# Source one-hots of the edge count split by columns between VectorE and ScalarE, beside a GpSimd scatter

## The reference

```
deg = segment_sum(ones, dst)                    # edges that end in each node
for k in 1, 2, 3:
    agg = segment_sum((feat * d_invsqrt)[src], dst)
    feat = feat - agg * d_invsqrt
    h = h + THETA[k] * feat
```

## Time and profile before

| | |
|---|---|
| median of 3 runs | 6393.17 us (6391.6 to 6401.1) |
| the profiled execution: its time, its span | 6387.14 us, 6385.3 us |
| TensorE matmul, weight load | busy 65% and 43% of the span |
| VectorE, ScalarE, GpSimd | busy 50%, 12% and 52% |
| scatter L440 | 784 instructions, 379.7 to 1493 us |
| counting | 419.5 to 931 us |

### The profile page before, as it was taken

How to read it: one execution, slowest core, us unless ns; L and a number is a source line. 1 busy time by engine, 2 the same in 40 slices (tenths; PEclk the granted TensorE clock), 3 DMA queues, 4 the chain that set the end, 5 groups by cost and what they waited for, 6 DMA issues and landing times. The chain is left out here.

```text
span 6385.3 us, 88933 instructions
## 1 busy us (share of the span) xinstructions
PE 4142.3 (65%) x19143; PEld 2771.2 (43%) x19144; DVE 3184.7 (50%) x7069; ACT 793.1 (12%) x2439; POOL 3315.9 (52%) x3323
## 2 busy tenths in 40 slices
PE   6969970003899788778746668888888844444431
PEld 5844430001499744444435534445445433333331
DVE  6966650005899456565566761122122255545556
ACT  1210000000110022222220010010010012222210
POOL 0048887772000077777733006737747547777761
PEclk7569985556899889898979979989999865555555
DMA  4311120001367577777745546767677643333331
GB/s 121 102 56 32 42 53 2 2 2 58 136 239 263 174 199 216 209 216 214 216 139 163 153 155 239 238 226 251 228 237 244 196 132 81 81 82 82 81 85 52
DMA packets 516122, 909.59 MB, mean 142 GB/s; under 512 B 100755, under 2 KB 349832, under 8 KB 476628
## 3 DMA queue, kind: packets, MB, share of 16 engines
q1 hardware_dynamic: 410094, 741.27, 35.7%
q0 software_dynamic: 105824, 165.90, 11.4%
HBM read 680.21 MB, written 226.65 MB: 142 GB/s over the span
## 5 line engine op out<-in xcount | busy, mean ns | idle before, releaser
L2768 POOL DMA_INDIRECT l_gathered<-l_table,l_st x816 | 775.6, 951 | 855.3 <-issue 782.0
L440 POOL DMA_INDIRECT by_src<-src_rec,src_pos x784 | 874.8, 1116 | 560.0 <-ACT attr_turned L742 321.2
L1790 POOL DMA_INDIRECT l_edges_by_src<-l_by_src,l_edges_st x816 | 786.7, 964 | 727.3 <-SPq L1884 478.9
L1790 POOL DMA_INDIRECT l_edges_by_src<-l_q,l_edges_st x816 | 778.4, 954 | 347.4 <-issue 242.9
L2837 PE MATMUL psum<-l_blocks,l_rows 128*128 128x512 f32 (+1 forms) x2016 | 814.7, 565 | 2.3 <-ACT l_rows L2779 2.3
L1869 PE MATMUL psum<-l_rows,l_edges_hot_t 128*128 x1632 | 443.1, 453 | 565.9 <-DVE l_scores L2907 542.6
L1688 PE MATMUL psum<-pair_hot_weight,pair_hot_dst 128*128 128x512 f32 x1200 | 642.9, 678 | 176.4 <-DVE pair_hot_dst L1678 165.6
L2796 DVE TENSOR_SCALAR l_hot<-iota,l_loc,l_weight 128x128 f32<-128x128 f32 x816 | 223.0, 360 | 916.8 <-PE psum L2853 913.6
L1869 PEld LDWEIGHTS psum<-l_rows,l_edges_hot_t 128*128 128x128 f32 x1632 | 379.0, 330 | 634.3 <-issue 634.3
L2837 PEld LDWEIGHTS psum<-l_blocks,l_rows 128*128 128x128 f32 x2016 | 373.5, 199 | 417.1 <-issue 412.3
L2504 PE MATMUL psum<-l_scaled,l_counts 128*128 128x128 f32 x3750 | 424.2, 277 | 18.8 <-ACT l_scaled L2429 18.8
(11 more groups left out here) (483 smaller groups left out, 5454.8 us busy)
## 6 DMA issues: line engine op xcount, KB each, us to landing
l_blocks<-pair_blocks SPq DMA_DIRECT2D x216, 1024.0 KB, 5.2
l_counts<-counts SPq DMA_DIRECT2D x65, 1600.0 KB, 6.8
pair_blocks<-pair_block SPq DMA_DIRECT2D x75, 1024.0 KB
l_edges_loc<-loc_by_tile SPq DMA_DIRECT2D x416, 128.0 KB, 3.0
l_rows<-l_edges_by_src SPq DMA_DIRECT2D x204, 256.0 KB
l_sum_rows<-l_rows SPq DMA_DIRECT2D x204, 256.0 KB, 2.6
attr_then_counts<-in_edge_attr SPq DMA_DIRECT2D x14, 1568.0 KB
counts<-attr_then_counts SPq DMA_DIRECT2D x13, 1600.0 KB
```

Source lines behind the costliest of these rows:

```text
L440: pool.indirect_dma_start(table, bass.IndirectOffsetOnAxis(ap=pos[:, e:e + 1], axis=0), rec[:, e, :], None).then_inc(s_out[g % R], 16)
L1790: pool.indirect_dma_start(a[:, r, g, :], None, table_src, bass.IndirectOffsetOnAxis(ap=st[:, r, g:g + 1], axis=0))\
L2768: pool.indirect_dma_start(sent[:, p, g, :], None, by_type, bass.IndirectOffsetOnAxis(ap=st[:, p, g:g + 1], axis=0))\
```

## The change

The 3200 columns of `hot_src` are shared out. VectorE writes the first 2048 (`WEIGHED = 16 * P`), with a compare whose result is multiplied by a column of ones, read per partition. ScalarE writes the other 1152 in two activations: the absolute difference between the column's number and the edge's source into a new f16 tile `apart`, then Relu of one minus that, which is 1 where the difference is 0 and 0 elsewhere. `apart` has one buffer: the second activation waits for the first by `s_apart`, the first for the second one of the tile before by `s_act`. Both engines wait for the place (`s_used`), and TensorE waits for both (`s_hot`, `s_act`). ScalarE gets the same loop over tiles, ahead of its row copies.

```diff
--- before.py
+++ after.py
@@ -813,6 +813,7 @@
 
     f16 = mybir.dt.float16
     HALF = NP // 2
+    WEIGHED = 16 * P
     node, wgt, rows, rows1 = edges
     with ExitStack() as ctx:
         key = k.sb(ctx, "src_key", [P, EC])
@@ -830,6 +831,8 @@
         iota = k.sb(ctx, "count_iota", [P, NP], f16)
         hot_src = k.sb(ctx, "hot_src", [P, places_ahead, NP + 1], BF16)
         hot_dst = k.sb(ctx, "hot_dst", [P, places_ahead, P], BF16)
+        apart = k.sb(ctx, "src_apart", [P, NP - WEIGHED], f16)
+        s_apart, s_act = k.sem("count_apart"), k.sem("count_hot_by_scalar")
         zero = k.sb(ctx, "count_zero", [1, PSUM_BANK], BF16)
         space = k.sb(ctx, "attr_then_counts", [P, 2 * 56 * 64])
         row = space[:, 0:NP]
@@ -898,11 +901,22 @@
             place = n % places_ahead
             v.wait_ge(s_used, n + 1)
             v.nop(nofuse=True)
-            v.tensor_scalar(hot_src[:, bass.ds(place, 1), 0:NP].rearrange("p a c -> p (a c)"), iota[:, :],
-                            shifted[:, 0, bass.ds(t, 1)], None, ALU.is_equal).then_inc(s_hot, 1)
+            v.tensor_scalar(hot_src[:, bass.ds(place, 1), 0:WEIGHED].rearrange("p a c -> p (a c)"), iota[:, 0:WEIGHED],
+                            shifted[:, 0, bass.ds(t, 1)], k.ones[:, 0:1], ALU.is_equal, ALU.mult).then_inc(s_hot, 1)
             v.tensor_scalar(hot_dst[:, bass.ds(place, 1), :].rearrange("p a c -> p (a c)"),
                             iota[:, bass.ds(b * P + KD * P, P)], shifted[:, 1, bass.ds(t, 1)], None, ALU.is_equal)\
                 .then_inc(s_hot, 1)
+
+        def one_hots_by_scalar(act, n, t):
+            act.wait_ge(s_used, n + 1)
+            act.wait_ge(s_act, n + 1)
+            act.nop(nofuse=True)
+            act.activation(apart[:, :], iota[:, WEIGHED:NP], ACT.Abs, bias=shifted[:, 0, bass.ds(t, 1)], scale=-1.0)\
+                .then_inc(s_apart, 1)
+            act.wait_ge(s_apart, n + 1)
+            act.nop(nofuse=True)
+            act.activation(hot_src[:, bass.ds(n % places_ahead, 1), WEIGHED:NP].rearrange("p a c -> p (a c)"), apart[:, :],
+                           ACT.Relu, bias=k.ones[:, 0:1], scale=-1.0).then_inc(s_act, 1)
 
         def vector(v):
             v.sem_inc(s_over, 1)
@@ -961,7 +975,12 @@
                     act.copy(tiles[:, f, h * PSUM_BANK:h * PSUM_BANK + n], k.ps[2 * f + h][:, 0:n]).then_inc(s_tile, 1)
             attr["scalar"](act)
             act.sem_inc(s_row, B)
+            act.wait_ge(s_ready, 1)
             with act.Fori(0, W - KD) as b:
+                first = act.value_load(first_i[0:1, bass.ds(b, 1)], min_val=0, max_val=TE - 1)
+                behind = act.value_load(behind_i[0:1, bass.ds(b, 1)], min_val=1, max_val=TE)
+                with act.Fori(first, behind) as t:
+                    one_hots_by_scalar(act, t + b, t)
                 for c, col, n in banks:
                     act.wait_ge(s_sum, b * B + c + 1)
                     act.nop(nofuse=True)
@@ -1005,6 +1024,7 @@
             pe.wait_ge(s_ready, 1)
             pe.wait_ge(attr["kept"], attr["groups"])
             pe.sem_inc(s_used, places_ahead)
+            pe.sem_inc(s_act, 1)
             pe.sem_inc(s_crow, B)
             with pe.Fori(0, W - KD) as b:
                 first = pe.value_load(first_i[0:1, bass.ds(b, 1)], min_val=0, max_val=TE - 1)
@@ -1017,6 +1037,7 @@
                     pe.matmul(k.ps[c][:, 0:n], zero[:, 0:P], zero[:, 0:n], start=True, stop=False)
                 with pe.Fori(first, behind) as t:
                     pe.wait_ge(s_hot, (t + b) * 2 + 2)
+                    pe.wait_ge(s_act, t + b + 2)
                     pe.nop(nofuse=True)
                     visit(pe, t + b)
                 for c, col, n in banks:
```

## The result

The changed kernel takes 6345.94 us (median of 4 runs, 6344.23 to 6355.6) against 6394.44 us of the kernel before (4 runs, 6391.6 to 6401.1): a ratio of 0.9926, 95% interval 0.9909 to 0.9943. It is 0.7% faster, where 1.1% was forecast. Its profiled execution took 6344.23 us, with a span of 6342.4.

What follows compares the result with a forecast made beforehand. The prediction took GpSimd's scatter to bound the stage: 123.5 us of stretching removed, 54 given back, 69 us less, so 6324 us, 1.1% faster. The range for 8 in 10 was 6262 to 6374 us.

Steps and rivals of the forecast that it cites:

- What bounds the stage: GpSimd's scatter, not the counting, sets the stage's end; counting costs it only 123.5 us by stretching scatters.
- Part 1: VectorE's compare and multiply of 2048 columns takes 0.82 us and still holds the port, giving back 54 us.
- Rival A: VectorE's f16 compare and multiply doesn't hold GpSimd's port; all 123.5 us go, 6270 us; chance 0.28.
- Rival B: VectorE's compare and multiply runs at the f32 pace, holding the port 1.06 us; 6445 us, slower; chance 0.05.
- The formula: Scatter's wait from a VectorE hold falling anywhere: hold squared over 1.26, 0.231 us a tile for 0.54 us.
- rival D: Scatter and counting rhythms lock, nearly every tile costs its whole hold, 110 us or more; 6380 and above; chance 0.09.
- Part 2: ScalarE's 1152 columns in two chained activations of 1229 ns, 0.2 us gaps; a tile of 2.86 us sets counting's pace.
- rival C: ScalarE's chain becomes the bound through 1283 ns table loads before both activations; 6760 us; chance 0.02.
- the slow clock: TensorE, idling between tiles, might fall to a granted clock of 0.50; seven products then take about 2.7 us.
- The cover: The scatter hides counting's 310 us of added time; this fails at a tile time of 3.4 us at the earliest.

Runs made afterwards that it cites:

- e9: Kernel before with series of wide VectorE instructions ahead of counting, series 2 by compare and multiply, series 3 by compare with accum_out; 7566.66 us against 7512.38.
- e7: The changed kernel, unchanged, on a chip with slow register instructions beside the scatter; 7719.52 us against 7508.76 for the kernel before, ratio 1.0278.
- e1: Changed kernel with VectorE's 2048 columns by a summing compare (accum_out) instead of the compare and multiply; ratio 1.0289 to the kernel before.
- e5: The kernel of e1 run once more, the summing compare in place of the changed kernel's compare and multiply; ratio 1.0290 to the kernel before.
- e11: Third run of the changed kernel with the summing compare in place of the compare and multiply; ratio 1.0292 to the kernel before.
- e12: Kernel before with eight series of VectorE turns of different lengths ahead of counting; scatter's extra 0.091 to 0.289 us a turn for 2048 columns.
- e6: The kernel before, unchanged, on a chip with slow register instructions beside the scatter; 7508.76 us.

## Why the prediction was right, and what it sized wrongly

**What bounds the stage: right.** The scatter sets the end before and after; the last one and the next block moved together by 50 us, with the counting over 243 us earlier.

**Part 1, length and form: right.** 0.817 us against 0.82. Rival A (0.28) is out: the form holds what the scatter needs, called the port here. The changed kernel's timeline shows the signature, and the bench the same 0.415 us with the multiply as without it. Rival B is out by the 0.817. The Trainium skill, in "SBUF — State Buffer", section "Who interferes with whom", counts tensor_scalar, but not its form that also writes out the accumulator, among the operations that can take the port pair which VectorE shares with GpSimd. Series 2 and 3 of e9 agree: 1094 ns for the scatter beside the compare and multiply, 958 beside the summing form.

**Part 1, the term of the sum that was mis-sized.** "0.54 x 0.54 / 1.26 = 0.231 us a tile", 54 us in all. Measured: 74.5 us, 0.30 a tile. The formula takes the hold to fall anywhere; at 2.90 us a tile it does not. Two scatters take 2.524 us, each pair is pushed into step by the hold, and a tile in step costs 2.90 - 2.524 = 0.37 us. By the records, 148 tiles follow one another at 2.8 to 3.0 us and cost 0.34 each, 50 us; the others cost 0.25 each, 24 us. Many of these stand at the start of a window, where VectorE does not wait and its compares come every 0.91 us (559.95, 560.86, 561.77), out of step.

The length of the hold was not at fault. Take each scatter from its recorded start and let it need the port 0.13 and 0.84 us into it, and let the wide instruction hold the port from 0.28 to 0.36 us after its start until its end, a hold of 0.46 to 0.54 us. That gives the 784 scatters' time (825.9 us) to within 2 us, and all but 8 of them to within 0.1 us, with nothing for ScalarE or TensorE. For the kernel before the same working is 32 to 45 us short, since some 40 scatters wait where it lets them pass: there a scatter that needs the port 0.23 us after the start of the compare is seen to wait for it, so the compare alone holds it sooner, for 0.82 us or more. Why the two forms differ in this was not looked into.

So rival D's mechanism was at work, with two scatters to a tile, which the prediction held to be less likely. Its price did not come: the step costs 0.37 and not the whole hold of 0.54. The forecast was 22 us low (6324 against 6346), and 20 of them are this term: with 74.5 in the place of 54 it would have been 6344. That the rest is so small is in part luck: the 6.6 us that are lost behind the stage in the profiled executions are nearly made up by where these two lie among their kernels' runs (6.0 us below the median before, 1.7 after).

**Part 2, ScalarE: right, a little short.** 1257 ns against 1229, gaps of 0.22 and 0.17 against 0.2, a tile of 2.90 against 2.86; counting ended at 1200, 30 us before the forecast, although the tile is longer: 245 x 2.90 and the 110 us of window ends would make 1240. The window ends are partly covered now, ScalarE and VectorE making the next window's first tiles while TensorE ends the last one (L918 at 558.28, L904 at 559.95, the window's first weight load at 561.41). No table load stands before either activation; rival C is out. TensorE's granted clock was 0.96 over the counting (0.94 before), although it now idles between tiles: the slow clock that the prediction allowed for did not come.

**The cover: right where it was read, and the step on which all hangs.** 562 us of room let 269 us of longer counting vanish. Where the register instructions are slow there is no room, the stage ends with the counting, and the same change costs 2.8%. The prediction named the tile time at which the cover fails, 3.4 to 3.9 us; there a tile takes 16.8 to 19.6 us beside the scatter in both kernels. It did not think of a chip on which the cover is not there before the change, and its direction, right for the first measurement, was wrong on the chip of e7.

**Open.** Why the instructions take 0.70 us there, and whether it is the chip or something else that differed, is not known. On such a chip the scatter ends at 1450 to 1456 whatever the form, the summing one too (a mean of 1043 to 1048 ns in e1, e5 and e11), although series 3 of e9 shows that form to cost nothing; something else stretches it, in periods of 1.40 us, and was not taken apart. That the summing form would give the kernel all of the 74.5 us back where register instructions are fast was not measured on the kernel itself, and neither were other borders there: that the rhythm gives the cost is shown by the series of e12 and the records of the changed kernel, not by a kernel with another tile time.

## What to carry to other kernels

- What a repeated hold costs a periodic stream of transfers depends on how the two periods stand to each other, not on the hold alone: work out the turn less a whole number of transfers (over one or two turns; the runs show three as well) that it can be pushed into, and take hold squared over period only where the turn is unknown.
- Work moved from the engine that disturbs the bound to one off the path is free only as far as its cover reaches. Say how long the cover is, and look at whether it is there on every chip: here the same change is 0.7% faster on one and 2.8% slower on another.

## What the runs showed of the hardware that was not expected

- In e1 to e11, on four chips, instructions came in steps of 0.70 us on the engine that set the pace while GpSimd issued its scatter: in e6 TensorE's register instructions took 699 ns instead of 46, and VectorE's of L901 took 702 to 1395 ns in the first nine tiles and 133 in most later ones; in e7 ScalarE's had a median of 48 ns at L914. So it was not every engine at once, as the expectation of e5 has it. In e9 VectorE's turns took 4.20 and 5.60 us, but its first nine, about 25 us, still ran at full pace. The kernel before took 1080 to 1135 us more on these chips, of which this stage has 411 in e6; the remainder lies in other stages.
- A compare and multiply in f16 with both numbers read per partition costs 60 ns more than the compare alone (0.815 against 0.755 us for 2048 columns, e9), and no more by column (1.117 against 1.057 for 3200).
- A compare with accum_out takes 2345 ns for 2048 columns, 2.9 times the compare and multiply, and leaves the scatter at 958 ns.
